# Gated two-expert block on one Trainium2 core: the first product of the routed blocks with the weights as the stationary operand

## The reference, cut to what matters

```python
def _swiglu(x, w1, w2, w3):
    return jax.nn.silu(x @ w1) * (x @ w2) @ w3
...
scores = jax.nn.sigmoid(x @ router_w)
_, top_idx = jax.lax.top_k(scores + expert_bias, K)          # K = 2 of E = 16
...
def body(acc, ws):
    w1, w2, w3, g = ws                                       # w1, w2: 256x256, w3: 256x256
    return (acc + _swiglu(xf, w1, w2, w3) * g[:, None], None)
routed_out, _ = jax.lax.scan(body, jnp.zeros_like(xf), (routed_w1, routed_w2, routed_w3, gf))
x = x + jnp.tanh(g_ffn[0]) * (shared_out + routed_out)
```

## Time and profile before

| what | value |
|---|---|
| median of three executions | 608.68 us (606.59 to 619.39) |
| the profiled execution, its time | 605.17 us |
| its span | 603.4 us |
| mean granted TensorE clock | 0.966 |
| PE busy | 556.8 us, 92% |
| DVE, ACT, POOL busy | 381.9, 251.1, 276.7 us |
| block stage, first to last start at L1467 | 273.8 to 469.2 us |

### The profile page before, as it was taken

The page is one execution under the profiler, slowest core; times in us unless marked ns, Lnnn a source line. Parts: engine busy times, 40 slices in busy tenths (PEclk is TensorE's granted clock), DMA queues, the critical chain, the costliest instruction groups (busy, mean ns, idle before and its releaser), DMA issues.

```text
span 603.4 us, 11604 instructions
## 1 busy us (share of the span) xinstructions
PE 556.8 (92%) x3334; PEld 359.2 (60%) x3335; DVE 381.9 (63%) x874; ACT 251.1 (42%) x546; POOL 276.7 (46%) x269
## 2 busy tenths in 40 slices
PE   4898898999999999909999999999999999999997
PEld 2565777764555666506666666666666555555554
DVE  1649989868887777615655555555555457664666
ACT  3456575663245665503333333333333323332322
POOL 1014555444357777764333333333331075751661
PEclk9798887999999999958999999999999999999999
DMA  8995233239332201012333333333342133370442
GB/s 217 285 335 175 105 111 132 112 133 287 114 115 62 70 5 33 0 55 89 106 104 104 105 104 104 105 104 105 104 104 78 45 97 113 97 243 19 131 125 85
DMA packets 52366, 69.72 MB, mean 116 GB/s; under 512 B 8256, under 2 KB 44416, under 8 KB 52336
## 3 DMA queue, kind: packets, MB, share of 16 engines
q1 hardware_dynamic: 42816, 48.41, 24.9%
q0 software_dynamic: 8944, 18.83, 11.6%
q10 hardware_dynamic: 576, 2.10, 1.1%
HBM read 46.30 MB, written 23.01 MB: 115 GB/s over the span
## 4 chain that ended last, share of the span: by engine, by line
PE 56%; POOL 15%; DVE 13%; issue 7%; DMA 4%; ACT 2%; SPq 1%; DVEq 0%; POOLq 0%; ACTq 0%
PE bank L1467 18%; PE bank L1384 14%; POOL slot_token L502 12%; PE bank L1405 8%; PE bank L1487 8%; PE bank L1456 3%; PE bank L1476 3%; POOL X L466 3%; DMA WR<-in_ctx_t 2%; DVE st L842 2%; DVE WR L814 2%; PE bank L1242 1%; DVE STAGE L861 1%; DVE WS L869 1%; DVE WR L832 1%
## 5 line engine op out<-in xcount | busy, mean ns | idle before, releaser
L1384 PE MATMUL bank<-XTC,WS 128*128 128x512 f16 x768 | 176.2, 379 | 0.0
L519 POOL DMA_INDIRECT ROWS<-xrow,idx x79 | 75.3, 953 | 115.7 <-PE bank L1456 110.3
L1467 PE MATMUL bank<-WR,XTB 128*128 x474 | 116.6, 382 | 5.2 <-DVE XTB L1121 4.3
L1384 PEld LDWEIGHTS bank<-XTC,WS 128*128 128x128 f16 x768 | 75.1, 98 | 76.9
L1405 PE MATMUL bank<-WS,GS 128*128 128x256 f16 x768 | 95.6, 275 | 4.5 <-POOL GS L485 2.2
L536 POOL DMA_INDIRECT ROWS<-yrow,posi x64 | 64.2, 1004 | 69.4 <-DVE X L1042 27.8
L1405 PEld LDWEIGHTS bank<-WS,GS 128*128 128x128 f16 x768 | 73.8, 99 | 31.0 <-DVE GS L1058 9.1
L1128 DVE SCALAR_TENSOR_TENSOR G<-bank,SIL 128x256 f32<-128x256 f32 x79 | 33.6, 425 | 84.3 <-ACT SIL L724 84.3
L502 POOL DMA_INDIRECT slot_token<-tokid,sloti x64 | 73.8, 1153 | 23.5 <-issue 19.2
L724 ACT ACTIVATE SIL<-bank 128x256 f32<-128x256 f32 x79 | 30.4, 384 | 122.8 <-PE bank L1467 122.8
L1052 DVE SCALAR_TENSOR_TENSOR G<-bank,SIL 128x512 f32<-128x512 f32 x63 | 43.5, 690 | 50.8 <-ACT SIL L668 50.7
(11 more groups left out here) (144 smaller groups left out, 688.7 us busy)
## 6 DMA issues: line engine op xcount, KB each, us to landing
yrow<-ROWS SPq DMA_DIRECT2D x79, 128.0 KB, 1.9
WR<-in_routed_w SPq DMA_DIRECT2D x39, 256.0 KB, 5.4
X<-in_x SPq DMA_DIRECT2D x4, 1024.0 KB, 14.0
xrow<-STAGE SPq DMA_DIRECT2D x8, 512.0 KB, 2.9
xtd<-STAGE SPq DMA_DIRECT2D x8, 512.0 KB, 2.6
out<-X SPq DMA_DIRECT2D x7, 512.0 KB, 5.2
WR<-in_ctx_t SPq DMA_DIRECT2D x4, 768.0 KB, 12.2
WR<-in_shared_w SPq DMA_DIRECT2D x3, 1024.0 KB, 15.7
```

The costliest lines, as they stand in the source:

```text
L519: pool.indirect_dma_start(out=XG[:, u, :], out_offset=None, in_=xrow, in_offset=bass.IndirectOffsetOnAxis(ap=idx[:, b:b + 1].bitcast(U32), ...
L1384: last = pe.matmul(acc[:, :], WS[:, wx, at:at + P], XTC[:, u, xx, k, :], start=(k == 0 and m == 0), stop=(k == KD - 1 and m == 2))
L1467: last = pe.matmul(bank[u][:, :], XTB[:, u, xx, k, :], w, start=(k == 0 and m == 0), stop=(k == KD - 1 and m == 2))
```

## The change

`block_hidden` changes the parts of the operands: a 128x128 slice of the weights is now stationary and the 128 columns of `XTB` move. The result comes out with the hidden dimension over the partitions, in four pieces of 128 columns of the same bank (two of w1, two of w2). For each piece and each half of the contraction there are three matmuls of 128 columns, 24 in all in place of six of 512. `hidden_transpose` is gone, with its semaphore `b_tg`: ACT and DVE read `G` itself (in SBUF) where they read bank 3. The silu, the gating and `block_rows` have the same shapes as before.

```diff
             def g_hi(b, u, first=False):
-                act.wait_ge(b_tg, b + 1)
+                act.wait_ge(b_g, b + 1)
                 if not first:
                     act.wait_ge(b_y, b - 1)
-                act.activation(GT[:, u, 0], bank[3][:, 0:RH].rearrange("p (k n) -> p k n", k=RH // P), ACT.Copy)\
+                act.activation(GT[:, u, 0], G[:, u, 0:RH].rearrange("p (k n) -> p k n", k=RH // P), ACT.Copy)\
                     .then_inc(b_ghi, 1)
...
             def gated(b, u, first=False):
                 dve.wait_ge(b_sil, b + 1)
                 if not first:
-                    dve.wait_ge(b_tg, b - 1)
+                    dve.wait_ge(b_glo, b - 1)
...
             def g_lo(b, u):
                 dve.wait_ge(b_ghi, b + 1)
-                dve.tensor_tensor(GT[:, u, 1], bank[3][:, 0:RH].rearrange("p (k n) -> p k n", k=RH // P),
+                dve.tensor_tensor(GT[:, u, 1], G[:, u, 0:RH].rearrange("p (k n) -> p k n", k=RH // P),
                                   GT[:, u, 0], ALU.subtract).then_inc(b_glo, 1)
...
                 if not first:
                     pe.wait_ge(b_g, b - 1)
-                for k in range(KD):
-                    hi = weights(e, k * 2 * RH, 2 * RH)
-                    lo = weights(e, WE + k * 2 * RH, 2 * RH)
-                    for m, (xx, w) in enumerate(((0, hi), (0, lo), (1, hi))):
-                        last = pe.matmul(bank[u][:, :], XTB[:, u, xx, k, :], w,
-                                         start=(k == 0 and m == 0), stop=(k == KD - 1 and m == 2))
+                for o in range(2 * RH // P):
+                    acc = bank[u][:, o * P:(o + 1) * P]
+                    for k in range(KD):
+                        hi = weights(e, k * 2 * RH + o * P, P)
+                        lo = weights(e, WE + k * 2 * RH + o * P, P)
+                        for m, (xx, w) in enumerate(((0, hi), (1, hi), (0, lo))):
+                            last = pe.matmul(acc, w, XTB[:, u, xx, k, :],
+                                             start=(k == 0 and m == 0), stop=(k == KD - 1 and m == 2))
                 last.then_inc(b_h, 1)
-
-            def hidden_transpose(b, u, first=False):
-                pe.wait_ge(b_g, b + 1)
-                if not first:
-                    pe.wait_ge(b_glo, b)
-                for k in range(RH // P):
-                    last = pe.transpose(bank[3][:, k * P:(k + 1) * P], G[:, u, k * P:(k + 1) * P], ident[:, :])
-                last.then_inc(b_tg, 1)
...
                         block_hidden(b, k % 2, es[k + 2])
-                        hidden_transpose(b - 1, (k + 1) % 2)
                         block_transpose(b + 2, (k + 2) % 4, i * 32 + 16 * ((k + 2) // 4 + h + 2))
                         block_rows(b - 2, k % 2, es[k])
```

More of the change, by code:

```diff
@@ L299, in flamingo_block @@
         b_g = sem("b_g")
-        b_tg = sem("b_tg")
         b_ghi = sem("b_ghi")
@@ L1175, in _ @@
             rows(NRUN - 2, (NRUN - 2) // 4, (NRUN - 2) % 4)
-            dve.wait_ge(b_tg, NRUN)
+            dve.wait_ge(b_glo, NRUN)
             gate_hidden(NSA, 0)
@@ L1502, in _ @@
                     pe.wait_ge(s_base, NCA)
-                if b >= 1:
-                    hidden_transpose(b - 1, (b - 1) % 2, b == 1)
                 block_transpose(b + 2, (b + 2) % 4, 16 * ((b + 2) // 4 + 1))
@@ L1520, in _ @@
                 block_hidden(b, b % 2, es[k + 2])
-                hidden_transpose(b - 1, (b - 1) % 2)
                 if b + 2 < NRUN:
@@ L1526, in _ @@
             hidden(NSA, 0, 0, load=NCA // 2 * 16 + 16)
-            hidden_transpose(NRUN - 1, (NRUN - 1) % 2)
             block_rows(NRUN - 2, (NRUN - 2) % 2, es[NRUN - 2 - (NBLK - 6)])
```

## The result

The changed kernel has a median of 672.64 us over four executions (671.33 to 674.10) against 607.63 us for the kernel before (four executions, 601.54 to 619.39). The ratio is 1.109, with a 95% interval of 1.104 to 1.115: slower by a tenth. The forecast was 670.0, in a range of 640 to 692.

The account below looks back on a forecast made before the run. PE's own stream bounds the kernel before; after the change its sequencer would: 1.94 + 1.49 - 0.13 + 0.02 = 3.32 us a block against 2.50, +0.82 x 79 = +64.8 on 605.2 gives 670.0 us, range 640 to 692.

Parts of the forecast that it names:

- the sequencer's address instructions set the pace: Block stage: PE's sequencer needs 3.32 us a block, above PE's own 2.19 to 2.86; PE idles a third; chance 0.74.
- The price of an address: Sequencer time for each run-time weight address in the hidden product: 0.124 us, twelve more adding 1.49 us a block.
- the 0.02 added: Sequencer's block: extra for the slightly longer step of a group's first address, raising 3.30 to 3.32 us.
- The room of 0.56 us in the sequencer: Kernel before: sequencer's semaphore waits at L1474 and L1482, 0.56 us a block, leaving 1.94 us of work in 2.50.
- the 0.13 for the dropped step: Sequencer's step at L1474, the wait for bank 3, removed with the transposes: about -0.13 us a block.
- p: First product on PE: one load and one float16 matmul of 128 columns, 0.055 to 0.083 us, 24 a block.
- The 81 ns of the Trainium skill: Skill page's sustained spacing for 128 columns with loads; PE's block would be 2.81 us, still below the sequencer's.
- Everything reaches the end: PE's stream ends the block stage and the shared expert does not overlap, so all +64.8 us lengthen the run.
- The clock and DVE as foreseen: Block stage: granted clock not under 0.9, DVE's steps as long as before; rival of a falling clock 748 us, chance 0.03.
- nothing is gained, since no PE stage waited for them: ACT and DVE in the block stage: reading G in SBUF and readying GT earlier brings no gain.
- rival A: Address instructions hidden at their recorded 46 ns, PE's block 2.30 us with stalls, faster at 589 us; chance 0.04.
- B: Rival: addresses hidden but load-matmul pairs not, p 0.083, PE's block 2.97 us, 642 us; chance 0.11.

Follow-up runs that it names:

- run 3: Changed kernel with one more load and matmul per pair of addresses, 32 products a block in place of 24, 16 addresses: 3.37 us a block, as without.
- run 4: Changed kernel with a third address for each piece, 24 addresses a block in place of 16, same 24 matmuls: 4.39 us a block, ratio 1.226 to the kernel before.
- run 2: Kernel before, x still stationary and transposes kept, moving weights in four pieces of 128 columns, 16 addresses, 24 matmuls: 3.51 us a block, ratio 1.114.
- run 5: Changed kernel with some or all lo parts at fixed addresses: 12 addresses 2.86 us a block, 8 addresses 2.52, against 3.37 with 16.
- run 1: Changed kernel with the first product's weights at fixed addresses, no address instructions there, same 24 matmuls: 2.48 us a block, ratio 0.989 to the kernel before.
- run 6: Kernel before without the transposes of the gated rows, ACT and DVE reading G: 2.51 us a block against 2.50, ratio 1.000.

## Why the prediction was right

- The cause: the sequencer's address instructions set the pace, the array waits. Shown by runs 3 and 4 from both sides, and by run 2 without the exchange of operands.
- The price of an address, 0.124 us: measured 0.128 (runs 4 and 5). The twelve cost 1.54 us in place of 1.49 and the 0.02 added. The record's own 46 ns would have said that nothing is lost.
- The room of 0.56 us in the sequencer and the 0.13 for the dropped step: 2.50 - 0.56 + 1.54 - 0.13 = 3.35, within 0.02 of the measured block. The dropped step is 0.14 by run 2. Worked back from the measured block, the sequencer of the kernel before needs 3.37 - 1.54 + 0.14 = 1.97 us, so its room was 0.53. The miss of 0.05 in the block is thus about half the room's and half the addresses'. The room had been read from two blocks to a tenth of a us; that it came out this close is partly luck.
- p, the load with its matmul: taken as 0.055 to 0.083, measured 0.056. The 81 ns of the Trainium skill (TensorE: Matmul & The Clock Gate, Back-to-back issue gap) do not fit this stream: 24 pairs in 1.34 us; the measurement decides. Nor does a load add to the step, though it fills all rows of the array.
- Everything reaches the end: +66.9 us in the stage, +67.2 in the span, against +64.8. Two small errors partly cancel: a block lost 0.87 in place of 0.82 us, but not all 79 lost that much, since 79 x 0.87 would be 68.7.
- The clock and DVE as foreseen: 1.00 in the window, and DVE's step to `GT` 415 ns in both kernels. ACT's step to `GT` did get longer, by 30 ns, when it read `G` in place of bank 3 (kernel before, then changed). It is not in the chain of waits of 320 to 346 us above.

```profile
L730 ACT ACTIVATE GT<-bank x79: 377/378/384, 278.5 to 473.5; 128x256 f16<-128x256 f32 x79
...
L729 ACT ACTIVATE GT<-G x79: 407/408/416, 278.8 to 538.2; 128x256 f16<-128x256 f32 x79
```

One step was wrong, without harm to the number: "nothing is gained, since no PE stage waited for them". PE's sequencer did wait for DVE, at L1482, and this wait was the next limit, at about 2.5 us a block. So rival A's price (2.30 us a block, 589 us) was false: even with the first product's addresses at no cost the changed kernel stands at 2.48 (run 1), no faster than before by more than 0.02. The prediction counted that wait as room and did not ask what it would be once PE's stream got shorter. B's price, 2.97, lies above that limit and is not touched by it; but its p of 0.083 is not the measured 0.056.

## What to carry to other kernels

Count the register instructions of TensorE's sequencer as a stream of their own beside the array's, at their spacing and not at their recorded length; exchanging operands to cut big moving operands into small stationary ones multiplies run-time addresses. Before taking work off the engine that looks bound, find the wait that comes next (here a single bank), and lift both together: without the transposes alone a block took 2.51 us, with the second banks alone 2.45, with both 2.36, against 2.50. The free time of the array was hidden in records that overlap.

## What was not expected

- PE's busy share stayed at 92% (19.1 of 20 us in the window) while the array had work for 2.2 of 3.37 us. The records of matmuls are 0.22 us long where they start every 0.056 to 0.09, so they cover gaps of a tenth. The "issue" idle ahead of the loads (35.8 us at L1468) also shows only part of the 1.15 us a block, 91 us in all, in which the array had nothing.
- The transposes' 0.21 us a block were worth nothing by themselves (run 6, ratio 1.000), although the busy shares and the chain of waits named PE as the bound.
- A float16 load of 128x128 hides behind a matmul of only 128 columns: 0.056 us a pair in run 1, at a granted clock of 1.00, where the record of the load alone is 0.10 long.
